# An attention block with a 4-bit gated feed-forward: the down projection by Strassen's seven products, with weight sums formed beside the gate and up matmuls

## The reference

```python
xn = (x - mean) / sqrt(var + 1e-5)                    # layer norm
# attention: 32 query heads, 8 key/value heads of width 32, rotary, causal
s = attention(xn @ wq, xn @ wk, xn @ wv) @ wo
# feed-forward: INTER = 2752; weights unpacked from 4-bit codes, scale * (code - zero)
inter = xn @ w_gu                                     # 2048 x 5504
h = silu(inter[..., :2752]) * inter[..., 2752:]
g = silu(h @ w_d)                                     # 2048 x 1024
out = x + s * g
```

## Time and profile before

| | |
|---|---|
| median of 3 runs | 2243.33 us (2243.0 to 2243.69) |
| profiled execution | 2242.64 us |
| its span in the profile | 2240.9 us |
| granted TensorE clock, mean | 1.00 of full speed |
| PE, DVE, POOL, ACT busy | 99, 55, 54 and 42% of the span |

### The profile page before, as it was taken

How to read it: one execution, slowest core, us unless ns; L and a number is a source line. 1 busy time by engine, 2 the same in 40 slices (tenths; PEclk the granted TensorE clock), 3 DMA queues, 4 the chain that set the end, 5 groups by cost and what they waited for, 6 DMA issues and landing times.

```text
span 2240.9 us, 38593 instructions
## 1 busy us (share of the span) xinstructions
PE 2220.2 (99%) x15048; PEld 1125.2 (50%) x15048; DVE 1221.9 (55%) x1951; ACT 930.6 (42%) x1806; POOL 1200.0 (54%) x1318
## 2 busy tenths in 40 slices
PE   7999999999999999999999999999999999999999
PEld 4555545555555555555555555444444444444444
DVE  5677677777777777777777763345312211112100
ACT  4333156666666666666666665332201000000000
POOL 4855588887887888788888876333301101001000
PEclk9999999999999999999999999999999999999999
DMA  7344212443424433334443233533273222313120
GB/s 208 97 105 100 50 33 57 72 76 55 67 59 81 72 67 59 67 62 72 76 61 61 66 53 61 94 103 92 81 295 127 100 91 77 113 64 127 45 89 19
DMA packets 266666, 188.03 MB, mean 84 GB/s; under 512 B 189728, under 2 KB 236318, under 8 KB 264052
## 3 DMA queue, kind: packets, MB, share of 16 engines
q1 hardware_dynamic: 266484, 185.56, 34.8%
HBM read 113.47 MB, written 71.90 MB: 83 GB/s over the span
## 4 chain that ended last, share of the span: by engine, by line
PE 98%; ACT 1%; DVE 0%; issue 0%; POOL 0%; DMA 0%; DVEq 0%; ACTq 0%; POOLq 0%
PE gu_ps L1174 39%; PE dn_ps L1731 19%; PE qk_ps L722 9%; PE out_ps L1717 7%; PE mx_ps L1071 6%; PE sc_ps L1115 6%; PE o_ps L1137 4%; PE v_ps L705 2%; PE o_ps L1141 2%; PE sz_ps L1084 2%; PE sz_ps L1089 1%; PE dn_ps L1726 1%; PE tr_ps L691 1%; ACT L1223 0%; POOL xl L412 0%
## 5 line engine op out<-in xcount | busy, mean ns | idle before, releaser
L1174 PE MATMUL gu_ps<-xT,wg 128*128 128x512 f16 x4128 | 983.6, 378 | 0.0
L1505 POOL TENSOR_TENSOR room<-room 128x1152 f16<-128x1152 f32 x256 | 539.5, 2107 | 40.3 <-ACT room L1223 26.4
L1174 PEld LDWEIGHTS gu_ps<-xT,wg 128*128 128x128 f16 x4128 | 367.8, 97 | 377.2 <-issue 0.7
L1223 ACT ACTIVATE room<-sc_ps 128x512 f32<-128x512 f32 (+3 forms) x768 | 349.3, 489 | 368.7 <-PE sc_ps L1115 365.0
L1731 PE MATMUL dn_ps<-xT,hT_in 128*128 128x512 f16 x1536 | 336.2, 379 | 0.0
L1899 POOL TENSOR_TENSOR room<-room 128x512 f32<-128x512 f32 x30 | 51.2, 1710 | 530.0 <-DVE room L1859 530.0
L1859 DVE TENSOR_TENSOR room<-room 128x512 f32<-128x512 f32 x32 | 23.9, 752 | 415.6 <-ACT room L1793 415.5
L1731 PEld LDWEIGHTS dn_ps<-xT,hT_in 128*128 128x128 f16 x1536 | 150.3, 98 | 181.2
L1500 POOL TENSOR_SCALAR_AFFINE_SELECT room<-room 128x128 f32<-128x128 f32 x512 | 144.8, 299 | 140.4 <-ACT room L1223 140.4
L1350 DVE TENSOR_REDUCE shift<-mx_ps 128x2 f16<-128x1024 f32 (+3 forms) x256 | 212.8, 831 | 8.8
L722 PE MATMUL qk_ps<-xT,w 128*128 128x512 f16 x960 | 212.8, 379 | 0.0
(11 more groups left out here) (124 smaller groups left out, 2551.6 us busy)
## 6 DMA issues: line engine op xcount, KB each, us to landing
hidden_scratch<-hT SPq DMA_DIRECT2D x84, 256.0 KB, 3.0
hT_in<-hidden_scratch SPq DMA_DIRECT2D x16, 1344.0 KB, 6.0
o_scratch<-room SPq DMA_DIRECT2D x64, 260.0 KB, 10.4
room<-o_scratch SPq DMA_DIRECT2D x16, 1040.0 KB, 8.1
arena<-q_scratch SPq DMA_DIRECT2D x48, 256.0 KB, 3.8
stock<-in_qw_d SPq DMA_DIRECT2D x42, 256.0 KB
down_scratch<-wd SPq DMA_DIRECT2D x84, 128.0 KB, 2.8
xin<-in_x SPq DMA_DIRECT2D x16, 512.0 KB, 4.6
```

Source lines behind the costliest of these rows:

```text
L1174: last = pe.matmul(to[:, :], wg[:, u, wp, s, cols], xT[:, xp, s, tokens], start=(s == 0 and k == 0), stop=(s == KT - 1 and k == 2))
L1223: act.activation(probs[:, r % 2, START[t] + c:START[t] + e], sc_ps[n % SC_BANKS][:, 0:e - c], ACT.Exp, scale=float(1.0 / np.sqrt(HD))).the ...
L1505: pool.tensor_tensor(p_lo[:, r % 2, c], probs[:, r % 2, c], p_hi[:, r % 2, c], ALU.subtract).then_inc(lo_done, 1)
```

## The change

**The down projection.** The 16 token tiles are taken in 8 pairs (n1, n2), the first 16 hidden tiles in 8 pairs (i even, i odd), and the columns in two halves. On this 2x2 block structure the eight block products are replaced by Strassen's seven. A `product` has 8 x 3 = 24 matmuls. The remaining 5 full tiles and the narrow one are multiplied as before by `rest`, 17 matmuls for each of the four outputs. The line numbers of the changed kernel for both are L1875, and L1864 and L1867.

**Weight sums.** Five of the seven products need a sum or difference of two weight blocks: 5 kinds x 8 pairs = 40 *items* of 128x512. They are formed two a step in steps 69 to 88, by the `tail` calls that now stand at several places (spots) in a step. An item takes two POOL operations (`bu`, L2180, the sum of the low parts; `bl`, L2184, the low part of the result), two DVE operations (`bt`, L2073, the sum of the high parts; `bsum`, L2064, the total) and one ACT copy (`bh`, the high part), all 128x512 with operands in SBUF. SP loads the source blocks from `down_scratch` and stores the items to `down_sum_scratch`, 256 KB each; in `finish` they are loaded again as blocks of 2 MB.

**Token sums.** Five products of a pair need a sum or difference of hidden tiles: `sum_tiles`, three DVE operations of 128x1024 in the single buffer `t`, then ACT's high part and POOL's low part into a ring of three.

**Order of the finish.** All 16 projections stand in front. Their results are stored to DRAM (`projected_scratch`, 512 KB a tile) and loaded again for the weigh. Outputs of products are put together in SBUF (`c`): per pair 4 ACT copies and 10 DVE additions of one PSUM bank each. Then silu, weigh and total as before.

The core of the diff:

```diff
                     select(m, r, i)
+                    if i in (2, 6):
+                        tail(dve, R * m + r, i // 4 + 1)
...
@@ -1544,18 +1557,22 @@
                 low(m, r, 0)
                 lows(*at(m, r, -1, R), 7)
                 hidden(*at(m, r, -1, R))
+                tail(pool, R * m + r, 1)
                 low(m, r, 1)
                 lows(m, r, 1)
+                tail(pool, R * m + r, 2)
                 low(m, r, 2)
                 lows(m, r, 3)
+                tail(pool, R * m + r, 3)
                 low(m, r, 3)
                 lows(m, r, 5)
                 tables(m, r)
+                tail(pool, R * m + r, 4)
...
+        ITEM_0 = LAST - 19
+        EARLY = 20
+        FREED = {B_M6: [(0, 1)], B_M7: [(1, 1)], B_M4: [(1, 0), (0, 0)]}
...
+            store_item(sp, g - 2)
+            store_item(sp, g - 1)
+            for own in (g, g + 1):
+                if is_item(own) and own % SUMS in FREED:
+                    sp.wait_ge(bt_done, own + 1)
+                    sp.wait_ge(bu_done, own + 1)
+                    for block in FREED[own % SUMS]:
+                        load_source(sp, own // SUMS + 1, block)
...
+            load_hidden(0)
+            load_hidden(1)
+            sp.dma_start(wk[:, :, :, :].rearrange("p h j c -> p h (j c)"), wd_d[:, :, PLAIN * D:(FTILES - 1) * D]
+                         ).then_inc(wk_loaded, 16)
+            load_whole(B_M5, 1, 1)
+            for h in range(2):
+                sp.dma_start(wd_c[h * FLAST:(h + 1) * FLAST, :], wd_d[0:FLAST, h, (FTILES - 1) * D:FTILES * D]
+                             ).then_inc(tail_loaded, 16)
             for n in range(TT):
-                m, u = n // 2, n % 2
-                load_sums(sp, m + 2, u)
-                load_hidden(m + 1, u)
-                store(m, u)
-                load_x(m + 1, u)
+                load_sums(sp, n + 4)
+                if n >= 1:
+                    store_sums(n - 1)
+                if n == 4:
+                    all_stored(sp, ITEMS)
+                    load_block(B_M3)
+                if n == 6:
+                    load_block(B_M1)
+            sp.wait_ge(a_turned, TT)
+            load_block(B_M4)
+            store_sums(TT - 1)
+            sp.wait_ge(out_ready, TT)
+            load_block(B_M7)
+            load_block(B_M6)
+            load_whole(B_M2, 0, 0)
+            for q in range(2):
+                sp.wait_ge(so_stored[q], 16 * TT // 2)
+            sp.wait_ge(last_zeroed, 2)
+            load_hidden(2)
+            load_last(0)
...
+            def rest(n, half, to, first, final):
+
+                cols, h = slice(half * BANK, (half + 1) * BANK), hT[n % 3]
+                for j in range(FTILES - 1 - PLAIN):
+                    for k, (hp, wp) in enumerate([(0, 0), (0, 1), (1, 0)]):
+                        pe.matmul(to, h[:, hp, PLAIN + j, :], wk[:, wp, j, cols],
+                                  start=(first and j == 0 and k == 0), stop=False)
+                for hp in range(2):
+                    last = pe.matmul(to, h[:, hp, FTILES - 1, :], wd_c[:, cols], start=False,
+                                     stop=(final and hp == 1))
+                return last
+
+            def product(to, stationary, kind, first=True, final=True):
+
+                for i in range(PAIRS):
+                    for k, (hp, wp) in enumerate([(0, 0), (0, 1), (1, 0)]):
+                        last = pe.matmul(to, stationary(hp, i), blocks[kind][:, wp, i, :],
+                                         start=(first and i == 0 and k == 0),
+                                         stop=(final and i == PAIRS - 1 and k == 2))
+                last.then_inc(m_done, 1)
...
+            def pair(p):
+                n1, n2, e, q = 2 * p, 2 * p + 1, 5 * p, SUMS * p
+                pe.wait_ge(ht_loaded[n1 % 3], 48 * (n1 // 3 + 1))
+                if p >= 1:
+                    pe.wait_ge(added, 10 * (p - 1) + 5)
+                rest(n1, 0, c_ps[C11], True, False)
+                rest(n1, 1, c_ps[C12], True, True).then_inc(k_done, 1)
+                if p == 0:
+                    pe.wait_ge(block_loaded[B_M3], 16)
+                free(e)
+                product(m_bank(e), lambda hp, i: hT[n1 % 3][:, hp, 2 * i, :], B_M3)
+                if p == 0:
+                    pe.wait_ge(block_loaded[B_M1], 16)
+                free(e + 1)
+                product(m_bank(e + 1), summed(q), B_M1)
+                if p == 0:
+                    pe.wait_ge(block_loaded[B_M5], 32)
+                free(e + 2)
+                product(m_bank(e + 2), summed(q + 1), B_M5)
+                if p == 0:
+                    pe.wait_ge(block_loaded[B_M7], 16)
+                product(c_ps[C11], summed(q + 2), B_M7, first=False)
+                if p == 0:
+                    pe.wait_ge(block_loaded[B_M6], 16)
+                else:
+                    pe.wait_ge(added, 10 * p)
+                product(c_ps[C22], summed(q + 3), B_M6, final=False)
+                if p == 0:
+                    pe.wait_ge(block_loaded[B_M4], 16)
+                pe.wait_ge(ht_loaded[n2 % 3], 48 * (n2 // 3 + 1))
+                free(e + 3)
+                product(m_bank(e + 3), lambda hp, i: hT[n2 % 3][:, hp, 2 * i + 1, :], B_M4)
+                if p == 0:
+                    pe.wait_ge(block_loaded[B_M2], 32)
+                free(e + 4)
+                product(m_bank(e + 4), summed(q + 4), B_M2)
+                rest(n2, 0, c_ps[C21], True, True).then_inc(k_done, 1)
+                rest(n2, 1, c_ps[C22], False, True).then_inc(k_done, 1)
...
+            for n in range(3):
+                project(n)
             units_done(pe)
+            for n in range(3, TT):
+                project(n)
-            project(1, 1)
-
-            def body(m):
-                for u in range(2):
-                    tile(m, u)
-                    project(m + 1, u)
-
-            bodies(pe, body)
-
...
+            for p in range(DP):
+                pair(p)
...
+            g = 2 * (k - ITEM_0) + spot - 2
+            if spot and is_item(g):
+                place_free(act, g)
+                act.wait_ge(bsum_done, g + 1)
+                act.activation(place(g)[:, 0, :], bt[g % 2], ACT.Copy).then_inc(bh_done, 1)
...
+            def copy(p, e, to):
+                k = [0, 1, 2, 5, 6][e]
+                act.wait_ge(m_done, 7 * p + k + 1)
+                if p >= 1:
+                    act.wait_ge(out_stored[to // 2], 16 * p)
+                bank = out_ps[(5 * p + e) % 4 // 2][:, (5 * p + e) % 2 * BANK:((5 * p + e) % 2 + 1) * BANK]
+                act.activation(c[:, to // 2, to % 2, :], bank, ACT.Copy).then_inc(copied, 1)
...
+        def item_sum(dve, g):
+
+            if is_item(g):
+                dve.wait_ge(bu_done, g + 1)
+                dve.wait_ge(bt_done, g + 1)
+                dve.tensor_tensor(bt[g % 2], bt[g % 2], place(g)[:, 1, :], ALU.add).then_inc(bsum_done, 1)
+
+        def item_high_parts(dve, g):
+
+            if is_item(g):
+                first, second, op = of_item(g)
+                operands(dve, g)
+                if g >= 2:
+                    dve.wait_ge(bl_done, g - 1)
+                dve.tensor_tensor(bt[g % 2], quarter(0, first), quarter(0, second), op).then_inc(bt_done, 1)
...
+            def sum_tiles(q):
+                if q >= SUMS * DP:
+                    return
+                first, second, op = of_sum(q)
+                for n in (first[0], second[0]):
+                    dve.wait_ge(ht_loaded[n % 3], 48 * (n // 3 + 1))
+                if q >= 1:
+                    dve.wait_ge(comb_lo, q)
+                dve.tensor_tensor(t[:, :, :], tiles(0, first), tiles(0, second), op).then_inc(comb_step, 1)
+                dve.wait_ge(comb_step, 3 * q + 1)
+                dve.tensor_tensor(t[:, :, :], t[:, :, :], tiles(1, first), ALU.add).then_inc(comb_step, 1)
+                dve.wait_ge(comb_step, 3 * q + 2)
+                dve.tensor_tensor(t[:, :, :], t[:, :, :], tiles(1, second), op).then_inc(comb_step, 1)
+
+            def add(p, number, to, bank, op):
+                if number > 1:
+                    dve.wait_ge(added, 10 * p + number - 1)
+                own = c[:, to // 2, to % 2, :]
+                dve.tensor_tensor(own, own, bank, op).then_inc(added, 1)
...
+            def pair(p):
+                q, n1, n2 = SUMS * p, 2 * p, 2 * p + 1
+                dve.wait_ge(m_done, 7 * p + 2)
+                dve.wait_ge(copied, 4 * p + 3)
+                add(p, 1, C22, of_m(p, 1), ALU.add)
+                sum_tiles(q + 3)
+                dve.wait_ge(m_done, 7 * p + 3)
+                add(p, 2, C11, of_m(p, 2), ALU.subtract)
+                add(p, 3, C12, of_m(p, 2), ALU.add)
+                dve.wait_ge(k_done, 3 * p + 1)
+                add(p, 4, C12, c_ps[C12], ALU.add)
+                sum_tiles(q + 4)
+                dve.wait_ge(m_done, 7 * p + 4)
+                add(p, 5, C11, c_ps[C11], ALU.add)
+                sum_tiles(q + 5)
```

(37 more changed lines are left out.)

513 lines of the change are left out of this document (305 added, 208 removed).

## The result

The changed kernel takes 2252.6 us (median of 5 runs, 2251.62 to 2253.82), the kernel before 2243.0 in the same rounds (2242.84 to 2243.69). The ratio is 1.0042, 95% interval 1.0028 to 1.0057: 0.4% slower, where 2228 and 0.7% faster was forecast.

What follows compares the result with a forecast made beforehand. PE alone was taken to set the time, busy 99%. Terms -41.4 + 24 + 1 + 0 + 1.4 = -15.0 us gave 2227.6, forecast as 2228 us; own range 2218 to 2238, 8-in-10 range 2204 to 2250.

Steps and rivals of the forecast that it cites:

- The matmuls removed: Down projection: 236 matmuls per pair of token tiles instead of 260, 192 fewer over 8 pairs at 0.216 us, -41.4 us.
- The pairs: Down products of token tile pairs: the tightest chain, M1's end to M6's start, leaves 1.6 us slack, so cost 0.
- the end: Last half of the finish: an addition before silu and one more wait of 0.69 us, +1.4 us.
- Rival E: Down products: token sum too late for M6 in each pair, 2248 to 2252 us; chance 0.06.
- narrow units: Four units holding 8 items: items set the pace, 7.9 us of POOL and DVE work in 5.2; 10 us taken.
- projection 2: Before the third projection: items 36 to 39 delay DVE's low part past its slack of 6.9 us, 7 us lost.
- the items' term: Weight sums beside units and projections: POOL and DVE block each other in SBUF, +24 us, bounds 0 and 54.
- the wide units: 15 units with two tails each: work just fits on average, queueing makes DVE late for rebuilds, 7 us.
- one tail in three: Wide units: assumed share of tail calls falling between two closely following rebuilds, 10 x 0.65 = 7 us.
- The sum of 42.5 in 44.1 us: Four wide units: mutually exclusive POOL and DVE work after 0.15 us back per operation, 96%, just fitting on average.
- Rival C: Units from step 69: lock held to each instruction's end, POOL and DVE set the pace, 2258 us; chance 0.10.
- the projections in front: Before projection 4: attention rows, loaded after other loads, are ready about when due; +1 us, bounds 0 and 4.

## Why the prediction was wrong, point by point

**Right.** The matmuls removed, -41.4: the account above closes with it. The pairs, 0: PE has no wait in them, M6 follows M7 without a gap, and 8 pairs with the end cost 1.6 more than their matmuls, of which 1.4 was forecast for the end. Rival E falls. The mechanism of the items was right in the main, with its place (DVE late for the rebuild, narrow units slow, a wait of 6.6 before projection 2): the blocked records show it, and the halves left out fit it. That the items' number paces the narrow units is not borne out: four fewer saved nothing there.

**The failed step, first part: the items' term, +24, measured 38.1** (29.9 up to projection 0 and 8.2 at projection 2). By parts: the wide units were put at 7 and lost about 17.5 (to 1615), the narrow ones and the last rebuilds at 10 and lost about 12.5, projection 2 at 7 and lost 8.2. So it was mostly the wide units, where I let one tail in three meet two close rebuilds. The sum of 42.5 in 44.1 us already was 96%, and I priced queues at such a load by a guess at single meetings; the records show the unchanged L1394 at three times its length. I had read the 96% as "it fits". At 68% by the same sum, one item a unit, 15 units cost 3.7 us, and 0.4 once the first source block was there in time. Rival C, the lock held to the end, would have been 54; the pair at 1461.58 above still fits the early release of the earlier trace rows. What came beside the port is the source blocks that DVE waited for, 10.2 us, which no term held: an item's wait for a DMA in DVE's queue stops the rebuild and the hidden product as much as one for POOL. 6.2 of the 17.5 us stand in the one unit behind the wait of 6.57. Without POOL's part the same place cost 2.6 behind 7.14, so the late block costs more where the port is loaded, and how much of the 6.2 is the block's alone stays open.

The Trainium skill, page "SBUF — State Buffer", section "SBUF: two separate sides", calls the shared pair an exclusive lock between GpSimd and DVE operations in a two-port mode or with two SBUF inputs. The trace agrees on the exclusion: `bt`, with two SBUF inputs, takes 0.68 us alone and 1.3 to 1.5 in the mean beside POOL, and the hidden product, which reads PSUM, keeps its 0.68. The runs with one half left out fit it (7 and 2 us alone, 30 together). For how long it is held the measurement decides: the blocked one starts 0.13 to 0.14 us ahead of the holder's recorded end.

**The failed step, second part: the projections in front, +1, measured 11.6** (8.9 at projection 4 and 2.7 of clock behind it). I took 8.1 MB at 413 GB/s, 19.6 us, from the moment SP is free. In the trace SP begins at 1675.7, and the rows land at 1703.3, 27.6 later: four issues held SP's queue for 8.51 + 4.90 = 13.4 us where the two behind them took 1.06. And SP began 42.4 later than before, while PE's projections were 38.1 late, since the last items and their stores stand in front. Moving the loads gave the 9 us back.

**What no term held: the clock.** 15.7 of the 49.7 us are matmuls at the lower clock behind PE's own waits. I had read the clock at full speed before and priced waits by their length alone. The gaps in the kernel before show the surcharge by itself. It is one cause inside both failed terms: without it they would be 34.0, against 25 forecast. So the waits alone were under-priced by 9 us, and 15.7 more come with the clock.

The range ended at 2250. Its upper part was built from cases of which one happens at a time; what happened was the items' term at 1.6 times its size, late loads, and the clock on both.

## What to carry to other kernels

A long matmul stream hides elementwise work only up to a load. In this kernel POOL and DVE exclude each other where both work in SBUF, so add their times up for each stretch, and don't take a sum just under the stretch for a fit: at 96% the wide units lost 17.5 us, at 68% 0.4 to 3.7. The sum is a warning and not a price, since two arrangements at 81 and 83% lost 32 and 29: there one engine's operations waited in the queue for the other's. Move the work to a stretch where one of the two is idle. A wait of TensorE can cost more than its length: behind the three longest gaps made here it was 1.7 to 2.6 us more. Look at what stands in an in-order queue behind each wait, and at how long an issue holds its queue. A change that loses 10 us can hide one that gains 33: leave out each half of the added work alone to see whether one engine's queue is at fault or the two together.

## What was not expected of the hardware

- TensorE's clock falls to 0.50 after waits of a few us. Idle gaps of 1.42 and 2.31 us left it at full speed; after 3.66, 5.00 and 7.24 us the next 48 matmuls lost 1.7, 2.6 and 1.9 us. Waits of 3.13 and 3.75 us in other runs cost nothing behind them.
- Two issues of 1 MB loads in rows of 1 KB held SP's queue for 8.5 us while other loads were under way, and for 2.75 us at another place.
- DVE's shift L1394 has one full SBUF operand and one of a single column, and is blocked by POOL like the operations with two full ones: 427 ns in the mean before, 1258 after.
